# Tap sums of a deformable convolution in 32x32 blocks over four PSUM banks, offsets projected by quarters, and a residual added by PE

## The reference

```python
x = x + L0(_gn(x))   # whitening: power iterations on 16x16 covariance blocks, then a 128x128 product
x = x + L1(_gn(x))   # deformable convolution (below)
x = x + L2(_gn(x))   # attention inside 64 windows of 7x7, then attention between the windows
x = x + L3(_gn(x))   # relu, a mask per channel, 3x3 convolution
```

```python
samp = bilinear(image, own place + grid[p] + offset[p])   # p = 0..8, per group
out  = sum_p softmax(mask)[p] * samp                      # then out @ out_w + out_b
```

## Time and profile before

| | |
|---|---|
| median of 3 runs | 11108.46 us (11075.77 to 11125.28) |
| the profiled execution's own time | 11137.82 us |
| its span in the trace | 11135.9 us |
| granted TensorE clock, mean over the span | 0.848 |
| PE, DVE, ACT busy | 80%, 66%, 33% |

### The profile page before, as it was taken

How to read it: one execution, slowest core, us unless ns; L and a number is a source line. 1 busy time by engine, 2 the same in 40 slices (tenths; PEclk the granted TensorE clock), 3 DMA queues, 4 the chain that set the end, 5 groups by cost and what they waited for, 6 DMA issues and landing times.

```text
span 11135.9 us, 288961 instructions
## 1 busy us (share of the span) xinstructions
PE 8908.2 (80%) x124030; PEld 4802.9 (43%) x124030; DVE 7395.0 (66%) x9080; ACT 3642.6 (33%) x5874; POOL 199.6 (2%) x254
## 2 busy tenths in 40 slices
PE   5478887887888888788888878888887888888887
PEld 5324444353443435344343534434354443435444
DVE  2476676667666776866677676667767766776663
ACT  0024333242333424233242433324243332424322
POOL 0000000000000000000000000000000000000000
PEclk7568798888978888897888989888898988889798
DMA  4001101111110111111011111101111010111101
GB/s 102 9 8 35 40 21 42 31 36 35 39 42 19 41 34 34 35 39 38 22 40 28 40 38 36 37 24 42 28 40 38 27 42 26 43 28 40 38 19 51
DMA packets 230314, 391.72 MB, mean 35 GB/s; under 512 B 25200, under 2 KB 166480, under 8 KB 221776
## 3 DMA queue, kind: packets, MB, share of 16 engines
q1 hardware_dynamic: 229008, 372.66, 12.0%
HBM read 192.47 MB, written 130.55 MB: 29 GB/s over the span
## 4 chain that ended last, share of the span: by engine, by line
PE 55%; DVE 25%; issue 12%; ACT 6%; DMA 1%; DVEq 0%; SPq 0%; POOL 0%; ACTq 0%; POOLq 0%
PE ps L875 10%; PE ps L743 7%; PE ps L678 7%; DVE arena L1679 4%; PE ps L776 4%; PE ps L751 4%; PE ps L792 3%; DVE arena L1656 3%; DVE arena L1662 3%; PE ps L974 3%; DVE arena L1739 3%; PE ps L964 3%; PE ps L765 2%; PE ps L700 2%; DVE arena L1645 1%
## 5 line engine op out<-in xcount | busy, mean ns | idle before, releaser
L875 PE MATMUL ps<-arena,ident 64*64 64x512 f32 x5600 | 2043.6, 763 | 965.9 <-DVE arena L1679 930.8
L877 PE MATMUL ps<-arena,ident 48*64 48x512 f32 x5600 | 2050.5, 764 | 0.0
L1679 DVE TENSOR_TENSOR arena<-arena 112x2560 f32<-112x2560 f32 x560 | 1573.4, 2817 | 0.5 <-PE ps L877 0.5
L875 PEld LDWEIGHTS ps<-arena,ident 64*64 64x64 f32 x5600 | 546.4, 163 | 2146.3 <-issue 2135.7
L743 PE MATMUL ps<-arena,wqk 128*128 128x400 f32 x2048 | 975.7, 602 | 175.1 <-DVE arena L1785 127.9
L1770 DVE COPY arena<-ps 128x400 f32<-128x400 f32 x512 | 293.2, 573 | 887.2 <-PE ps L743 886.0
L678 PE MATMUL ps<-vp,convw 128*128 128x448 f32 x2016 | 816.9, 550 | 23.6 <-ACT vp L1287 23.6
L1662 DVE TENSOR_TENSOR arena<-arena 112x576 f32<-112x576 f32 x1008 | 764.0, 758 | 34.9
L776 PE MATMUL ps<-ident,arena 128*128 128x128 f32 x4096 | 620.3, 300 | 206.7 <-ACT arena L1215 57.4
L792 PE MATMUL ps<-arena 64*64 64x33 f32 x32768 | 674.6, 235 | 106.9 <-issue 69.9
L751 PE MATMUL ps<-wv,arena 128*64 128x256 f32 x4096 | 657.7, 447 | 107.3 <-ACT arena L1158 95.5
(11 more groups left out here) (286 smaller groups left out, 12294.3 us busy)
## 6 DMA issues: line engine op xcount, KB each, us to landing
windows_out<-arena SPq DMA_DIRECT2D x1024, 100.0 KB
arena<-windows_out SPq DMA_DIRECT2D x224, 256.0 KB, 4.1
arena<-windows_out SPq DMA_DIRECT2D x224, 192.0 KB, 3.3
arena<-in_wqk SPq DMA_DIRECT2D x16, 2048.0 KB, 8.4
arena<-in_x_t SPq DMA_DIRECT2D x16, 1568.0 KB, 10.3
arena<-in_x SPq DMA_DIRECT2D x16, 1568.0 KB, 6.7
arena<-arena SPq DMA_DIRECT2D x32, 784.0 KB
out_x<-xb SPq DMA_DIRECT2D x112, 224.0 KB, 1.9
```

The source lines that it names most:

```text
L875: nc.tensor.matmul(ps[half, 3, :], ident[0:SLOT, 0:SLOT], prod[0:SLOT, ring(c, dy), dx, :], start=(s < 2), stop=(s >= TAPS - 2), skip_grou ...
L877: mm = nc.tensor.matmul(ps[half, 4, :], ident[SLOT:PT, SLOT:], prod[SLOT:PT, ring(c, dy), dx, :], start=(s < 2), stop=(s >= TAPS - 2), ski ...
L1679: V.tensor_tensor(prod[0:PT, ring(c, dy), :, :].rearrange("p k (n e) -> p k n e", e=CG), taps.to_broadcast([PT, SHIFTS, N64, CG]), for_tap ...
```

## The change

1. **Tap sums.** The rows are cut into four blocks of 32 (the last has 16), and tap s writes column quarter s mod 4. Row block r sums in bank r, so banks 0 to 3 hold the sums. `taps_sum` copies four banks, and `turn_sum` adds four quarters for each row block: 16 matmuls of up to 32 columns in place of 8 of up to 64.
2. **Offsets of tiles 1 to 6** are projected one pixel column (a quarter, `t`) at a time into bank 5, which they share with `turn_sum` and `project_out`, and ACT copies each to SBUF (`copy_offsets`, 432 columns). This happens two tiles ahead, at `dy` 3 and 4 of tile c for tile c+2; tile 1's four quarters stand at the head of the stage. The softmax's shift (`later_shift`), the exponential (`later_exp`) and the hats (`later_hats`) read SBUF and take a whole tile in one instruction each where there were two. Tile 0 is as before.
3. **Window projection.** PE adds the residual `xb` by an identity product in front of L974's four, ACT adds the bias and writes `xb` back (`windows_added`); DVE's add L1877 is gone.
4. **Order.** Attention between windows and aggregation come two to three half steps earlier (aggregation from q 20, not 22), in banks 4, 6, 7. DVE adds a convolution chunk (`ADD_Q`) three half steps later than before, the last ones bunched at the end.

The diff, cut to its core (bank numbers and the waits that follow from them are left out):

```diff
+TOK_Q, TURN_Q, Q2_Q, S2_Q, SOFT_Q, A2_Q, AGG_Q = 2, 6, (8, 10), 12, 15, 18, 20
+STAT_LAG = 6
+GN_Q = AGG_Q + 13 + STAT_LAG
+CONV_Q = [GN_Q + 9 + j for j in range(3 * CHUNKS)]
+ADD_Q = [min(at + 4, 2 * TR * SHIFTS - 7 + k) for k, at in enumerate(CONV_Q[2::3])]
...
-            def project(n, c, half):
+            def project(n, c, t):
                 pe.wait_ge(y1_g.sem, y1_g.at(n, c + 1))
-                pe.wait_ge(of_h.sem, of_h.at(n, 2 * c + half))
-                pe.wait_ge(of_s.sem, of_s.at(n, 2 * c + half))
-                project_bias(0, 6)
-                project_bias(1, 7)
-                project_tile(n, c, 2 * half, 6)
-                project_tile(n, c, 2 * half + 1, 7).then_inc(of_p.sem, 1)
+                if t or c == 2:
+                    pe.wait_ge(lq_s.sem, lq_s.at(n, 4 * (c - 1) + t))
+                elif c == 1:
+                    pe.wait_ge(of_h.sem, of_h.at(n))
+                    pe.wait_ge(of_s.sem, of_s.at(n))
+                else:
+                    pe.wait_ge(rs_s.sem, rs_s.at(n, c - 2))
+                project_bias(t, 5)
+                project_tile(n, c, t, 5).then_inc(lq_p.sem, 1)
 
             def sum_taps(n, c, dy):
...
-                    half = slice(s % 2 * SLOT, (s % 2 + 1) * SLOT)
-                    nc.tensor.matmul(ps[half, 3, :], ident[0:SLOT, 0:SLOT], prod[0:SLOT, ring(c, dy), dx, :],
-                                     start=(s < 2), stop=(s >= TAPS - 2), skip_group_check=True)
-                    mm = nc.tensor.matmul(ps[half, 4, :], ident[SLOT:PT, SLOT:], prod[SLOT:PT, ring(c, dy), dx, :],
-                                          start=(s < 2), stop=(s >= TAPS - 2), skip_group_check=True)
+                    quarter = slice(s % 4 * 32, s % 4 * 32 + 32)
+                    for r in range(4):
+                        rows = slice(32 * r, min(32 * r + 32, PT))
+                        mm = nc.tensor.matmul(ps[quarter, r, :], ident[rows, 32 * r:32 * r + 32],
+                                              prod[rows, ring(c, dy), dx, :],
+                                              start=(s < 4), stop=(s >= TAPS - 4), skip_group_check=True)
                 mm.then_inc(pr_u.sem, 1)
...
                 for t in range(T4):
-                    nc.tensor.matmul(ps[:, 5, t * PT:t * PT + SLOT], total[:, 0, t * C:(t + 1) * C], stack[:, :],
-                                     start=True, stop=True)
-                    mm = nc.tensor.matmul(ps[:, 5, t * PT + SLOT:(t + 1) * PT], total[:, 1, t * C:(t + 1) * C],
-                                          stack[:, 0:PT - SLOT], start=True, stop=True)
+                    for r in range(4):
+                        at, count = t * PT + 32 * r, min(32, PT - 32 * r)
+                        mm = nc.tensor.matmul(ps[:, 5, at:at + count], total[:, r, t * C:(t + 1) * C], stack[:, 0:count],
+                                              start=True, stop=True)
...
+                nc.tensor.matmul(ps[:, 4, 0:WS * SLOT], ident, xb_win[:, :, nb, :, :].rearrange("c X Y j -> c j X Y"),
+                                 start=True, stop=False)
                 for m in range(4):
-                    mm = nc.tensor.matmul(ps[:, 2, 0:WS * SLOT], wout[:, m, :], ag[:, m, :], start=(m == 0), stop=(m == 3))
+                    mm = nc.tensor.matmul(ps[:, 4, 0:WS * SLOT], wout[:, m, :], ag[:, m, :], start=False, stop=(m == 3))
...
             def last_tiles(n):
                 sum_taps(n, TR - 1, SHIFTS - 1)
+                pe.wait_ge(nf_s.sem, nf_s.at(n))
                 turn_sum(n, TR - 1)
...
+            def copy_offsets(n, c, t):
+                act.wait_ge(lq_p.sem, lq_p.at(n, 4 * (c - 1) + t + 1))
+                act.wait_ge(rw_s.sem, rw_s.at(n, c))
+                nc.scalar.activation(om_later[0:PT, :].rearrange("p (q t g) -> p q t g", t=T4, g=G1)[:, :, t, :],
+                                     ps[0:PT, 5, 0:OFFS].rearrange("p (q g) -> p q g", g=G1), ACT.Copy
+                                     ).then_inc(lq_s.sem, 1)
+
+            def later_hats(n, c):
...
+                act.wait_ge(lq_s.sem, lq_s.at(n, 4 * c))
+                act.wait_ge(k_s.sem, k_s.at(n, 3 * c))
+                nc.scalar.activation(h[1], offs, ACT.Abs)
+                nc.scalar.activation(h[2], offs, ACT.Relu)
+                own.step(nc.scalar.activation(h[0], offs, ACT.Relu, scale=-1.0))
+                own.step(nc.scalar.activation(offs, h[1], ACT.Relu, bias=neg1[0:PT, :], accum_out=near[0:PT, c + 1:c + 2]))
+                nc.scalar.activation(h[1], h[1], ACT.Copy, scale=-1.0, bias=1.0).then_inc(lh_s.sem, 1)
...
             def taps_sum(n, c):
                 act.wait_ge(pr_u.sem, pr_u.at(n, (c + 1) * SHIFTS))
+                act.wait_ge(oo_p.sem, oo_p.at(n, c))
...
-                nc.scalar.activation(total[:, 0, :], ps[:, 3, :], ACT.Copy)
-                nc.scalar.activation(total[:, 1, :], ps[:, 4, :], ACT.Copy).then_inc(sum_s.sem, 1)
+                nc.scalar.activation(total[:, 0:2, :], ps[:, 0:2, :], ACT.Copy)
+                nc.scalar.activation(total[:, 2:4, :], ps[:, 2:4, :], ACT.Copy).then_inc(sum_s.sem, 1)
...
+            def later_shift(n, c):
+                logits = logits_of(c)
+                dve.wait_ge(lq_s.sem, lq_s.at(n, 4 * c))
+                ownm.step(V.tensor_reduce(mx1[0:PT, :], logits.rearrange("p (q n) -> p n q", q=P9), AX.X, ALU.max))
+                V.tensor_tensor(logits.rearrange(by_tap, q=P9), logits.rearrange(by_tap, q=P9), per_pixel(mx1), ALU.subtract
+                                ).then_inc(lm_s.sem, 1)
```

274 lines of the change are left out of this document (155 added, 119 removed).

## The result

The changed kernel takes 11366.17 us (median of 4 runs, 11344.81 to 11394.17), the kernel before in the same comparison 11116.87 us (4 runs): ratio 1.0232, 95% interval 1.0192 to 1.0271. It is 2.3% slower; the prediction was 10750 us and "faster".

What follows compares the result with a forecast made beforehand. PE and DVE were taken to bound the kernel by turns, both waiting in tile stages. Fifteen stages -330, sample 0 -35, last tail +6 gave 10777 us in the span, 10750 as median; 8-in-10 range 10600 to 11030.

Steps and rivals of the forecast that it cites:

- 105.1 becomes 100: -5: Tiles 2 and 3, PE's: turns and ACT's pieces cost, an earlier aggregation start gains more; together 5 us shorter a stage.
- Tap group 1.9 to 2.1 us: Sign for PE's tap sums in 32-row blocks: a group takes this at the full clock, wrong from 2.4 us.
- rival 2: Tap sums: the small blocks don't overlap, four at once make a group 4.5 us and the kernel 11750 us; chance 0.10.
- `turn_sum` 3.7 us: Sign for turning a tile's tap sum on PE: 32 passes take 3.7 us, +13 us a stage.
- Identity product +6, doubled if the stride costs: Window projection: two more PE passes in each of 7 windows, 6 us a stage; a dear strided operand adds 6 more.
- 20 projection passes at no more than 0.41 us: Offsets' projection: its price within PE's work of a tile, 21.7 us in all at the full clock.
- Sample 0's tiles 34 to 35 us: Sign for sample 0, nothing woven in: tiles fall from 41.0 us as DVE's waits for projection and exponential go.
- at the 0.67 of that tile it is 32 us, still under DVE's 34: Sample 0's tile: PE's 21.7 us of work, stretched by the low clock, stays below DVE's; low stretches cost DVE some 2 us.
- Tile 1 49.6 to 39.5, tile 4 +2: DVE's tiles: tile 1 loses 10 us of waits and moved products; tile 4's group norm pass stands behind ACT's hats.
- In a step PE has 1.96 + 4.09: Tiles 2 and 3: tap group plus window projection, in place of 2.79 + 3.27 us, nothing gained beside the unchanged aggregation.
- Tiles 5 and 6, -12: Deferred adds stop starving PE, taps -8, turns +5.6, half projection -2.6: the two tiles go from 105.2 to 93 us.
- Rival 3, the clock gives it back: Less work lowers the clock to 0.85 in tiles 2, 3, 5, 6, some 19 us a stage, about 11050 us; chance 0.10.
- Rival 1, ACT: ACT becomes the neck: PE stands behind its long pieces in tiles 2, 3, 5, 6, 14 us a stage, about 10960; chance 0.22.

Runs made afterwards that it cites:

- bias112: Changed kernel with each later offset projection's one-row bias product replaced by one of 112 rows, same result and passes: 11081 us, ratio 1.0024.
- dveadd: Changed kernel with the third part undone: no identity product, DVE adds projected window, bias and residual: 11208 us, ratio 1.0119.
- b64_b112_dve: Changed kernel with tap sums in 64x64 blocks, bias products of 112 rows and the residual added on DVE: 10925 us, ratio 0.9868.
- late_adds: Kernel before with only DVE's adds of the convolution chunks moved three half steps later, the last ones bunched: 10955 us, ratio 0.9897.
- warm: Changed kernel plus 14 unread full-array products a stage, after tap sums in tiles 0 and 4: 11407 us, ratio 1.0303.
- oldq: b64_b112_dve with attention between windows and aggregation put back to the half steps of the kernel before: 10875 us, ratio 0.9825.

## Why the prediction was wrong

It had the tile stage at 336 us, and it took 376.4. Two steps failed, and each made about half of the 40 us.

The first is that **PE's low clock was taken as covered by DVE, and the clock itself as given**: in tiles 0, 1 and 4 and in sample 0. With biases of 112 rows and nothing else changed (bias112) 18 us a stage came back, and tiles 0, 1, 4, 5 and 6 then took 42.8, 41.7, 56.7 and 95.8 (5 and 6 together) where 42, 39.5, 58.6 and 93 were forecast.

The second is **"105.1 becomes 100: -5"** for tiles 2 and 3. They took 122.0 us in the mean, and 121.2 with the biases repaired, so this is not the biases' clock. PE's work in them rose from 87.7 to 93.9 us at the full clock. The identity product accounts for 4 us of time (dveadd: 117.7); the rest is shown only in part.

Its steps, by its own numbers:

- *Tap group 1.9 to 2.1 us*: 2.15 at the full clock, against 2.79. All 16 blocks do work side by side; rival 2 is out. Work -26 for -29. Its first 16 passes start within 0.10 us (timeline of PE, 4137.85 to 4138.05):

```profile
4137.91 0.71 PE L889 MATMUL ps<-arena,ident 32*32 32x512 f32 x16
```

- *`turn_sum` 3.7 us*: 3.64, and +12 a stage for +13. Right.
- *Identity product +6, doubled if the stride costs*: the doubled case, +11.
- *"20 projection passes at no more than 0.41 us"*: 16 of them are the four quarters, and at 1.88 us each these take 7.5 us a tile, 0.47 a pass and not 0.41. The larger fault is that their difference to the two halves of 2.62 before was in no sum of the tile stage: +12 us of work. So PE's work came out at +6 where the sum had -10.
- *Sample 0's tiles 34 to 35 us*: 37.6. Here the step that failed is **"at the 0.67 of that tile it is 32 us, still under DVE's 34"**. The load itself came out as forecast: PE was busy 32.8 of the 37.6 us, at 0.68. What was wrong is "still under", as if a sum below DVE's were cover. At half the clock the turn (7.0 us), the quarters (3.5 us each with a copy behind it) and the taps (3.9 us) come one behind the other, and DVE, which has two buffers, waited 22.0 us of the stage for them. With 64x64 blocks and 112-row biases the tile took 33.9 us, and the stage 233 us where 243.5 was forecast. The mechanism was right, its cover was not.
- *Tile 1 49.6 to 39.5, tile 4 +2*: 53.9 and +6.3 in the medians. Same cause: with biases of 112 rows they take 41.8 and 56.7 us, near the forecast. In tile 1 DVE's new wait is that for the attention's product L935, 10 us a stage, and 4 with those biases; the prediction doesn't name it.
- *Tiles 2 and 3, -5*: +16 (105.3 to 121.7). 9.6 of this came back in tile 3 without the identity product, 4.3 of it lost again in tile 2 (dveadd); the earlier places of aggregation cost 7.1 of the two tiles' 115.1 us in b64_b112_dve, though in the changed kernel they helped. That leaves the larger part without a run of its own. "In a step PE has 1.96 + 4.09" was in fact 2.15 + 5.02 (1.83 + 3.19).
- *Tiles 5 and 6, -12*: -8.6, and the late adds alone give it (late_adds).
- *Rival 3, the clock gives it back*, was the nearest, with the wrong reason and the wrong place. It let less work lower the clock, and work rose. I priced it in PE's tiles at 0.85 (19 us lost a stage). It fell there too (0.93 to 0.87 in tile 3, 0.98 to 0.90 in tile 6), but most of it lay in DVE's tiles 0, 1 and 4 (means 0.76 to 0.60, 0.80 to 0.69, 0.71 to 0.57), where a low clock looked free because PE had waited. With tiles 2 and 3 on top, it did not stop at "same".
- *Rival 1, ACT*: PE's waits for ACT in the stage shown add up to 17 us (9.0, 5.6, 2.2, 0.6), but the mark was 10 us in tap groups or aggregation, and there it is the 5.6 of aggregation: under the mark. The largest part, 9.0, stands behind the quarters' copies. When ACT's hats were moved in b64_b112_dve, only 0.2 points came off.
- *The range of its own*: "turning free, -190" would put its lower end at 10560, not 10620, and rivals 2, 4 and the far half of 3 add up to 0.21, not to under 0.2. Neither bears on the outcome.

What stays open: what else lengthens tiles 2 and 3, why the granted clock of tiles 3 and 5 fell when work was added elsewhere (warm), and why the window stages became 3.7 us shorter (in late_adds, with its one edit, 2.7 us: part of it is that of the late adds). The part behind the last tile got 10 us longer for the 6 forecast.

## What to carry to other kernels

Split PE's busy time into work at the full clock and clock before a change in the form of matmuls is priced, and price each new form at both levels: here +6 us of work came with +39 us of busy time. An engine's slack in another engine's tiles is no free cover if it holds only at the upper clock. And try the pieces of a large change alone: the late adds were 1.0% by themselves, and the best version (oldq: 64x64 blocks, 112-row biases, DVE's adds, offsets ahead, old places) is 1.75% faster than the kernel before (interval 1.2 to 2.3), with parts 1 and 3 and the places of part 4 taken out again.

## What the runs showed of the hardware

- A product of one row is dear beyond its passes: as many passes of 112 rows in its place took a stage's clock over PE's work from 0.79 to 0.86 and 2.1 points off the time.
- Blocks of 32x32 work side by side (40 passes of 512 columns in 2.15 us), and yet the kernel with 64x64 blocks, which take 2.79, was faster in both pairs of runs (1.0232 and 1.0098; 0.9920 and 0.9868), at a higher clock (0.814 and 0.848; 0.844 and 0.869). How much of that is the form of the blocks and how much the added work is not told apart.
- fp32 columns strided by 7 elements took 1.83 us for two passes of 448 where contiguous ones took 1.02.
